# Turning derived token quarters on TensorE instead of by DMA in a fused attention and feed-forward kernel

## What is computed

```python
xn = _layernorm(x)
s = _L0_attn_ref(xn, Wq, Wk, Wv, bias_table, gamma, beta)
h = jnp.square(jax.nn.relu(jnp.einsum('bsd,fd->bsf', xn, W_fc)))
y = jnp.einsum('bsf,df->bsd', h, W_proj)
g = _silu(spikes_counted_over_5_steps(y) / 5)
out = x + s * g
```

## Time and profile before

| | us |
|---|---|
| median of 3 runs | 3989.05 |
| the profiled execution | 3991.72 |
| its span, first to last instruction | 3989.8 |
| TensorE busy (matmul) | 3409.3 (85%) |
| VectorE busy | 2798.7 (70%) |
| ScalarE busy | 2721.0 (68%) |
| GpSimd busy | 1867.6 (47%) |

### The profile page before, as it was taken

How to read it: one execution, slowest core, us unless ns; L and a number is a source line. 1 busy time by engine, 2 the same in 40 slices (tenths; PEclk the granted TensorE clock), 3 DMA queues, 4 the chain that set the end, 5 groups by cost and what they waited for, 6 DMA issues and landing times.

```text
span 3989.8 us, 62988 instructions
## 1 busy us (share of the span) xinstructions
PE 3409.3 (85%) x22284; PEld 1680.2 (42%) x22284; DVE 2798.7 (70%) x4812; ACT 2721.0 (68%) x4411; POOL 1867.6 (47%) x1094
## 2 busy tenths in 40 slices
PE   7566788666667787689999999999999999999996
PEld 4344455444444554445343434343434343434331
DVE  8445666554555665556778788878787888787877
ACT  6233333322223333236999999999999999999997
POOL 4021222121212221115997767576767676767672
PEclk9788898888888888889999999999999999999999
DMA  5544354444443444443132323232323222323232
GB/s 202 152 134 129 108 171 144 138 139 134 141 127 111 145 151 135 140 140 122 38 96 96 112 70 91 91 91 70 112 70 112 71 90 91 91 72 110 71 90 75
DMA packets 334024, 446.07 MB, mean 112 GB/s; under 512 B 175472, under 2 KB 211056, under 8 KB 333712
## 3 DMA queue, kind: packets, MB, share of 16 engines
q1 hardware_dynamic: 315280, 324.61, 27.0%
q10 hardware_dynamic: 18432, 117.45, 8.7%
HBM read 284.75 MB, written 83.95 MB: 92 GB/s over the span
## 4 chain that ended last, share of the span: by engine, by line
ACT 30%; PE 10%; issue 9%; DVE 3%; DMA 1%; SPq 0%; ACTq 0%; POOL 0%; DVEq 0%; POOLq 0%
ACT recurrence_or_probs L1865 16%; ACT s_sb L1872 15%; PE misc L1739 3%; PE acc L1814 2%; PE s_ps L1794 2%; PE s_ps L1780 2%; DVE s_sb L1941 2%; DMA xT<-xnT 1%; PE misc L1721 1%; DVE gate_or_tokens L2070 0%; SPq L319 0%; DVE outT L1961 0%; DVE x_or_queries L1978 0%; DVE gate_or_tokens L2073 0%; PE s_ps L1739 0%
## 5 line engine op out<-in xcount | busy, mean ns | idle before, releaser
L1941 DVE TENSOR_SCALAR_CACHE_REDUCE s_sb<-s_ps 128x1024 f32<-128x1024 f32 x998 | 1214.3, 1221 | 354.2 <-PE s_ps L1780 326.9
L2147 POOL TENSOR_TENSOR recurrence_or_probs<-recurrence_or_probs,toep 128x512 f32<-128x512 f32 (+1 forms) x375 | 1288.8, 3457 | 366.1 <-ACT recurrence_or_probs L1865 365.8
L1872 ACT ACTIVATE s_sb<-s_sb,nmax 128x1024 f32<-128x1024 f32 x998 | 1166.1, 1168 | 9.8 <-DVE s_sb L1941 9.4
L1865 ACT ACTIVATE recurrence_or_probs<-s_ps 128x1024 f32<-128x1024 f32 x1024 | 1060.3, 1037 | 6.8 <-PE s_ps L1794 6.4
L950 ACT ACTIVATE snap<-ps_fc 128x256 f32<-128x256 f32 x384 | 147.5, 384 | 1012.3 <-PE ps_fc L715 1011.0
L732 PE MATMUL ps_y<-w_pr,hid_part 128*128 128x512 f16 x3072 | 831.6, 388 | 0.0
L1814 PE MATMUL acc<-recurrence_or_probs,val 128*32 128x512 f32 x4096 | 545.8, 605 | 1.6 <-DVE recurrence_or_probs L2057 1.5
L715 PE MATMUL ps_fc<-recurrence_or_probs,w_fc 128*128 128x256 f16 x1536 | 224.4, 285 | 240.0 <-DMA recurrence_or_probs<-x_or_queries 209.9
L715 PE MATMUL ps_fc<-xnS_part,w_fc 128*128 128x256 f16 x1536 | 222.7, 284 | 221.5 <-DMA xnS_part<-x_or_queries 184.0
L732 PEld LDWEIGHTS ps_y<-w_pr,hid_part 128*128 128x128 f16 x3072 | 306.7, 100 | 184.0 <-issue 11.3
L1191 DVE BATCH_NORM_STATS2 stats<-x_or_queries 128x6 f32<-128x512 f32 x64 | 40.9, 682 | 488.7 <-DMA x_or_queries<-in_x 488.7
(11 more groups left out here) (202 smaller groups left out, 4388.2 us busy)
## 6 DMA issues: line engine op xcount, KB each, us to landing
w_fc<-fc_made ACTq DMA_DIRECT2D x120, 896.0 KB, 5.1
toep<-table_rows SPq DMA_DIRECT2D x32, 2048.0 KB, 8.4
x_or_queries<-x_or_queries SPq DMA_DIRECT2D x384, 64.0 KB, 2.0
x_or_queries<-in_x SPq DMA_DIRECT2D x16, 1024.0 KB, 6.7
xnT<-xnT_part SPq DMA_DIRECT2D x32, 512.0 KB, 11.8
x_or_gate<-in_x SPq DMA_DIRECT2D x16, 1024.0 KB, 6.6
base<-x_or_gate SPq DMA_DIRECT2D x16, 1024.0 KB, 10.7
xT<-xnT SPq DMA_DIRECT2D x32, 512.0 KB, 9.7
```

Source lines behind the costliest of these rows:

```text
L1865: nc.scalar.activation(prob[:, k % PROBS, 2 * second:2 * second + 2, :].rearrange("p j n -> p (j n)"), s_ps[:, item_buffer(pair_item(m)), ...
L1872: nc.scalar.activation(s_sb[:, i % 4, :], s_sb[:, i % 4, :], ACT.Exp, bias=nmax[:, par, j, st:st + 1], scale=-1.0, accum_out=den[:, par, j ...
L1941: nc.vector.tensor_scalar(s_sb[:, i % 4, :], s_ps[:, item_buffer(tile_item(n)), :], -1.0, None, ALU.mult, ALU.min, accum_out=nmax[:, par, ...
L2147: nc.gpsimd.tensor_tensor(tile, tile, toep[:, par, :, at:at + width], ALU.add).then_inc(biased, 1)
```

## The change

The turns of chunks 1 to 15 are no longer split and then turned by 32 transfers, but turned as float32 by TensorE into the two `ps_t` banks, and split as they are read out of PSUM. A quarter (`turn_quarter`) is four transposes into one bank. Steps 4 and 5 of a chunk take two quarters each for the next chunk (steps 6 and 7 in chunk 0): one ahead of product 2, one ahead of product 5. ScalarE's `copy_turned` writes the hi part straight into `xnS`, in `after_second` and `after_fourth`; VectorE's `turned_lo` the lo part, behind `combine(n, 1)` and behind `combine(n, 2)`. `product(n, 2)` of a chunk waits for these. `take_bank` makes TensorE wait until the last reader of a bank is done. The fetch of x for chunks 2 to 15 moves from SyncE's queue to ScalarE's (`fetch_x`, in `after_second` of step 5, ahead of `snapshot(n, 2)`), where it waits until TensorE has read all four quarters of the chunk before. Turning transfers for `xnT` stay. Left out of the diff: names and semaphores that are only removed.

```diff
--- before.py
+++ after.py
...
 WEIGH_LAG = 3
+TURN_AT = {c * 8 + 4 + 2 * (c == 0) + h: (c + 1, 2 * h) for c in range(15) for h in range(2)}
 FIRST_TILES = 2 * (SLOT_STEPS - TILE_LAG)
...
 QKV_LO_AT = {23: 0, 30: 1, 31: 2}
-TURNS_AT = ({4: (0, 1), 5: (2, 3)}, {3: (0, 1), 4: (2, 3)})
-TURNS_LO_AT = ({5: (0, 1), 6: (2, 3)}, {4: (0, 1), 5: (2, 3)})
 GATES_AT = ({4: (0,), 5: (1,), 6: (2,)}, {4: (0,), 6: (1, 2)})
...
         self.turns = shared[:, 0].rearrange("p a n -> p (a n)").rearrange("p (j t n) -> p j t n", j=4, t=2)
-        self.turn_part = half(1).rearrange("p (a j t n) -> p a j t n", a=2, j=4, t=2)
         self.nat = half(0).rearrange("p (w a s) -> p w a s", w=2, a=2)
...
         turns = first.turns
         xnT = sb("xnT_part", [P, 2, 2, EB, 512], F16)
...
         xn_lo = sem("xn_lo")
         xt_turned = sem("xt_turned")
         xt_stored = sem("xt_stored")
...
                     sp.wait_ge(xs_ps, 4)
-                elif c > 1:
-                    sp.wait_ge(turn_hi, (c - 1) * 4)
-                    sp.wait_ge(turn_lo, (c - 1) * 4)
                 sp.dma_start(x_in[:], d["x"].rearrange("(c t p) e -> c p t e", p=P, t=4)[c]).then_inc(x_loaded, 16)
...
                                          transpose=True).then_inc(xt_turned, 16)
-                if c == 1:
-                    sp.wait_ge(fc_lo, 8)
-                for part, done in ((0, turn_hi), (1, turn_lo)):
-                    for j in range(4):
-                        sp.wait_ge(done, (c - 1) * 4 + j + 1)
-                        for t in range(2):
-                            for k in range(2):
-                                sp.dma_start(xnS[par][:, part, j, k, t * P:(t + 1) * P], turn_part[:, part, j, t, k * P:(k + 1) * P],
-                                             transpose=True).then_inc(xs_turned, 16)
...
                     turn(c + 1, 1 - par)
-                if c < NC - 2:
-                    load_x(c + 2)
                 if c == 0:
...
                     sp.wait_ge(xt_turned, (NC - 1) * TURNED)
-                    sp.wait_ge(xs_turned, (NC - 1) * TURNED)
+                    sp.wait_ge(xs_ps, NC * 4)
                     first.stack(sp, first.nat, first.qst, first.kst)
...
         def _(pe):
+            last_read = [None, None]
+            def take_bank(i):
+                if last_read[i]:
+                    pe.wait_ge(*last_read[i])
+            def turn_quarter(c, j):
+                take_bank(j % 2)
+                pe.wait_ge(turns_made, c * 4 + j + 1)
+                for k in range(2):
+                    for t in range(2):
+                        at = k * HALF + t * P
+                        last = nc.tensor.transpose(ps_t[:, j % 2, at:at + P], turns[:, j, t, k * P:(k + 1) * P], ident[:])
+                last.then_inc(xs_ps, 1)
+                last_read[j % 2] = (xs_lo, c * 4 + j + 1)
             def column_sums(n):
...
                     pe.wait_ge(normed[QKV], 1)
+                if n >= 8:
+                    take_bank(bank[n])
+                    last_read[bank[n]] = (normed[QKV], n - 7)
                 for c in range(4):
...
                 elif i == 2:
-                    if n == 0:
-                        pe.wait_ge(xs_hi, 4)
-                        pe.wait_ge(xs_lo, 4)
-                    elif p == 0:
-                        pe.wait_ge(xs_turned, c * TURNED)
+                    if p == 0:
+                        pe.wait_ge(xs_hi, c * 4 + 4)
+                        pe.wait_ge(xs_lo, c * 4 + 4)
                     pe.wait_ge(snapped, n * 4 + 1)
...
                     pe.wait_ge(first_loaded, 64)
-                wait(pe, first.qk_read, q - 1)
+                take_bank(q % 2)
+                last_read[q % 2] = (first.qk_read, q + 1)
                 which, half = w["q" if q < 2 else "k"], q % 2
...
                 first_tile(n, 0)
+                if n in TURN_AT:
+                    turn_quarter(TURN_AT[n][0], TURN_AT[n][1])
                 product(n, 2)
...
                 proj(b, 1)
+                if n in TURN_AT:
+                    turn_quarter(TURN_AT[n][0], TURN_AT[n][1] + 1)
                 product(n, 5)
...
-            def turned_hi(c, j):
+            def copy_turned(c, j):
                 if j == 0:
-                    act.wait_ge(turns_made, c * 4 + 4)
-                    act.wait_ge(xn_lo, c * 4)
-                nc.scalar.activation(turn_part[:, 0, j], turns[:, j], ACT.Copy).then_inc(turn_hi, 1)
+                    wait(act, multiplied, (c - 1) * PAIRS * PRODUCTS)
+                    if c == 1:
+                        act.wait_ge(fc_lo, 8)
+                act.wait_ge(xs_ps, c * 4 + j + 1)
+                nc.scalar.activation(xnS[c % 2][:, 0, j].rearrange("p k s -> p (k s)"), ps_t[:, j % 2, :], ACT.Copy).then_inc(xs_hi, 1)
+            def fetch_x(c):
+                act.wait_ge(xs_ps, c * 4)
+                nc.scalar.dma_start(x_in[:], d["x"].rearrange("(c t p) e -> c p t e", p=P, t=4)[c]).then_inc(x_loaded, 16)
...
                 if q == 0:
-                    act.wait_ge(turn_lo, (NC - 1) * 4)
+                    act.wait_ge(xs_ps, NC * 4)
                 nc.scalar.activation(first.nat[:, which, 0, half * 512:(half + 1) * 512], ps_t[:, q % 2, :], ACT.Copy,
...
                     spiking.sigmoid(c - 1, p - 3, 1)
+                if n in TURN_AT:
+                    copy_turned(TURN_AT[n][0], TURN_AT[n][1])
+                    if TURN_AT[n][1] and TURN_AT[n][0] < NC - 1:
+                        fetch_x(TURN_AT[n][0] + 1)
                 if n in QKV_AT:
...
                     store_quarters(n + 1)
-                if c < NC - 1 and p in TURNS_AT[c > 0]:
-                    for j in TURNS_AT[c > 0][p]:
-                        turned_hi(c + 1, j)
+                if n in TURN_AT:
+                    copy_turned(TURN_AT[n][0], TURN_AT[n][1] + 1)
                 if n in SQUARE_AT:
...
                         dve.wait_ge(turns_made, 4)
-                    wait(dve, xs_turned, (c - 1) * TURNED)
+                    wait(dve, turns_made, c * 4)
                 nc.vector.tensor_scalar(xn[:, t, :], x_in[:, t, :], mv[:, t, 0:1], rs[:, 6, t:t + 1],
...
             def turned_lo(c, j):
-                dve.wait_ge(turn_hi, (c - 1) * 4 + j + 1)
-                nc.vector.tensor_tensor(turn_part[:, 1, j], turns[:, j], turn_part[:, 0, j], ALU.subtract).then_inc(turn_lo, 1)
+                dve.wait_ge(xs_hi, c * 4 + j + 1)
+                nc.vector.tensor_tensor(xnS[c % 2][:, 1, j].rearrange("p k s -> p (k s)"), ps_t[:, j % 2, :],
+                                        xnS[c % 2][:, 0, j].rearrange("p k s -> p (k s)"), ALU.subtract).then_inc(xs_lo, 1)
...
                     part_lo(c + 1, 1)
-                if ahead and p in TURNS_LO_AT[c > 0]:
-                    for j in TURNS_LO_AT[c > 0][p]:
-                        turned_lo(c + 1, j)
+                if n in TURN_AT:
+                    turned_lo(TURN_AT[n][0], TURN_AT[n][1])
                 if n in QKV_LO_AT:
...
                 combine(n, 2)
+                if n in TURN_AT:
+                    turned_lo(TURN_AT[n][0], TURN_AT[n][1] + 1)
                 if n == 0:
```

More of the change, by code:

```diff
@@ L341, in feed_forward @@
         turns = first.turns
-        turn_part = first.turn_part
         xnT = sb("xnT_part", [P, 2, 2, EB, 512], F16)
@@ L406, in feed_forward @@
         xn_lo = sem("xn_lo")
-        turn_hi = sem("turn_hi")
-        turn_lo = sem("turn_lo")
         xt_turned = sem("xt_turned")
-        xs_turned = sem("xs_turned")
         xt_stored = sem("xt_stored")
```

## The result

The kernel after takes 3522.98 us, the median of four runs (3521.45 to 3525.17), against 3988.62 us of the kernel before beside it (3987.89 to 3991.13): a ratio of 0.8832, 95% interval 0.8817 to 0.8847. That is 465.6 us less. The profiled execution's span is 3521.0 us, 468.8 less than before.

What follows compares the result with a forecast made beforehand. TensorE was taken to be held by waits for transfers into `xnS` at chunk starts. A + B + C = 498 us gained, D + E + F + G = 52 added: 446 less than 3989.05, 3543 us; range 3512 to 3600.

Steps and rivals of the forecast that it cites:

- A: At the start of chunks 1 to 15, TensorE's 15 waits for transfers into `xnS` go: 393.9 us less.
- B: At 14 chunk starts, TensorE's wait behind VectorE's stand for x goes, x being fetched earlier: 54.8 us less.
- C: Behind the idle time at 15 chunk edges, slow matmuls at a lowered clock go: 49.5 us less.
- The 12 us of slack: The 32 `xnT` transfers that stay land some 12 us before the next chunk's product 0 reads them.
- Term D: 16 float32 transposes a chunk on TensorE, 15 chunks, all on the path: 26 us added, upper end 65.
- (1): At product 0 the `xnT` transfers become late, 4 us per chunk plus clock loss: 120 us more, 3663 us; chance 0.09.
- (2): In ScalarE's queue the x fetch holds up weights, or a longer hold costs 5 us a chunk: 3613 us; chance 0.05.
- (3): In step 4 TensorE stands 42 us for GpSimd's turns, 14 times: slower than before, 4131 us; chance 0.02.
- (4): The chunk's edge waits for something else as late as `xnS`: about 3989 us; chance 0.02.
- Term E: In step 5 ScalarE's fetch of x holds snapshot 2 and so product 5: 1.2 us, 14 times, 17 us added.
- Term F: In chunk 1, whose x is fetched together with three weight loads, one wait stays: about 4 us (0 to 10).
- Term G: TensorE's 0.71 us wait behind VectorE's step 4 subtractions may vanish (-15 us) or recur in a second step (+18); taken +5.

Runs made afterwards that it cites:

- turning_16_more: The kernel after with 16 more turning transfers a chunk behind the 32 for `xnT`, product 0 waiting for them too: 3640.17 us, ratio 0.9123.
- x_early_alone: The kernel before with only its fetch of x moved to ScalarE's queue, in step 6 (7 in chunk 0): 3913.69 us, ratio 0.9803.
- fetch_sync: The kernel after with the fetch of x back on SyncE's queue, behind the transfers for `xnT`: 3499.61 us, ratio 0.8767.
- quarters_twice: The kernel after with each quarter turned twice on TensorE, 8 transposes instead of 4: 3548.86 us, ratio 0.8889.
- fetch_late: The kernel after with the fetch of x still on ScalarE's queue, but issued behind snapshot 2 of the step: 3510.01 us, ratio 0.8794.
- turning_8_more: The kernel after with 8 more turning transfers a chunk behind the 32 for `xnT`, product 0 waiting for them too: 3522.39 us, ratio 0.8823.
- before_sub_behind: The kernel before with the second of VectorE's two subtractions moved behind combine 2: 3986.46 us in one run, beside 3988.91 of the kernel before.

## Why the prediction was right, and where it was off

The forecast was 3543 us and the time is 3522.98, 20 us less, inside the range.

**Terms A, B and C** (498.2 us) came as reckoned: no wait for `xnS` or `xnT`, no stand of VectorE for x in chunks 2 to 15, a granted clock of 1.00 at the edges. The 12 us of slack given to `xnT` are some 15: the 32 transfers leave by 605.48 and product 0 starts at 622.07, while in `turning_16_more` product 0 starts 1.3 us behind the end of the last transfer's issue. The prediction counted the landing from that end; the 2.9 us of the earlier trace rows count from the start of the issue. Two reasons were incomplete. The prediction put term B down to the fetch two steps ahead on ScalarE's queue. That is enough by itself (`x_early_alone`), but so is removing the 32 transfers (`fetch_sync`), and the change did both. And C was put down to idle time as a whole; `x_early_alone` shows that about a third of it hung on the second stand. The sum is the same, since both waits went.

**Term D** was 26 us and is 26: the quarters are 0.44 us each on the path by `quarters_twice`. The row of transposes in a row was the right one to take, not the duration of one. The page's 275 ns (the Trainium skill, TensorE: Matmul & The Clock Gate, Part 4: PE-mode transpose) agrees with the 272 to 273 ns of each of the 240 here and says nothing of how closely they follow each other.

**The rivals** stayed away: no wait for `xnT` (1), no row for a weight transfer among the waits of TensorE (2), no wait for the turns (3), and the 15 waits did go (4). 1 and 3 were made to happen above, at 7.0 and 7.5 us a chunk.

**Term E** was 17 us and is 16. ScalarE's timeline at the hold:

```profile
598.98 0.40 ACTq L924 DMA_DIRECT2D x_or_queries<-in_x  x1
599.48 0.38 ACT L960 ACTIVATE snap<-ps_fc 128x256 f32<-128x256 f32 x1 [2.93 <-PE ps_t L627]
```

The fetch is issued as quarter 3 ends, the snapshot follows at 599.48, product 5 at 599.92. Without the hold product 5 would start 0.43 us after the quarter does, at 598.77; it starts 1.15 us later, 14 times. `fetch_late` confirms it: without the hold its chunks are 79.87 us long, 1.15 less.

**Term F** was 4 us and is 8.5. Chunk 1, in TensorE's timeline:

```profile
120.38 0.82 PE L713 MATMUL ps_fc<-recurrence_or_probs,w_fc 128*128 128x256 f16 x6
...
127.33 1.46 PE L713 MATMUL ps_fc<-recurrence_or_probs,w_fc 128*128 128x256 f16 x6 [5.49 <-DVE u L1311]
...
133.39 0.82 PE L713 MATMUL ps_fc<-xnT_part,w_fc 128*128 128x256 f16 x6
```

and in VectorE's, where the statistics wait for x:

```profile
126.26 0.69 DVE L1204 BATCH_NORM_STATS2 stats<-x_or_queries 128x6 f32<-128x512 f32 x1 [7.31 <-DMA x_or_queries<-in_x]
```

The wait is 5.49 us, and the products behind it run slow: from product 2 (120.38) to product 5 (133.39) are 13.01 us, where an undisturbed step has 4.55, so 2.97 are slow matmuls. The prediction counted the wait and left out the clock behind it. x is issued among SyncE's weight loads, as foreseen, and takes 12 us to land instead of the 6.7 of the earlier trace rows; in `turning_8_more`, where these loads leave 10 us later, it lands in 5.9; the transfers' engines are busy all the time there (share 1.00 in the first line of the stretches above). ScalarE's queue:

```profile
114.16 0.46 ACTq L924 DMA_DIRECT2D x_or_queries<-in_x  x1
```

**Term G** is the step that was mis-sized. The prediction took +5 us, between "may shrink to nothing (-15)" and "recur in a second step (+18)". It shrank to nothing: the chunk of 81.02 us is eight steps (78.12), four quarters (1.74) and the hold with its tail (1.15), and nothing more. 14 chunks of 1.16 us are -16. The prediction had one of the two causes, the moved subtraction, and left out the other: TensorE's own added work ahead of product 1 gives VectorE 0.87 us to catch up. The first is shown by `before_sub_behind`; the second follows from its numbers and was not tried alone. The high end, a second pause, had no row behind it.

D + E + F + G = 26 + 16 + 8.5 - 16 = 34.5 instead of 52, and 498.2 - 34.5 = 463.7 us, against 465.6 between the medians and 468.8 between the spans. The 2 to 5 us that remain are not placed. So the 20 us between forecast and result are G (21 us too high), against which F (4.5 us too low) happens to work, and this rest.

## What to carry to other kernels

Work added to the engine that sets the time isn't lost in full where that engine pauses for another one: take the pause off before the addition is counted. A transfer that waits for the engine that sets the time doesn't belong into another engine's program ahead of work for which the first one waits in turn: the same fetch behind that work was 13 us cheaper, and from SyncE's queue, with x of chunk 1 in time as well, 23. And when a queue is shortened, look at what stands behind the removed entries: here the x fetch would have come early by itself (`fetch_sync`).

## What the runs showed of the hardware

- Turning transfers of 32 KB follow each other by 1.3 to 1.4 us in one queue, however few there are (16 in 22.77 us, 8 in 10.22, 32 in 42.37); regular ones of 64 KB took 0.67 us each (24 in 16.00).
- Four float32 transposes of 128 x 128 cost 0.43 us among other matmuls, although each lasts 0.27, and the granted clock stayed at 1.00 with 16 of them in a chunk (540 to 625 us).
- In chunk 6 a second stand of 4 us soon behind one of 26.70 us left the granted clock at 0.56 in the 6.7 us behind it; without it the clock was 0.77 in the first 5.8 us behind the long stand and 1.00 in the next 8. Over 14 chunks such second stands cost 15.5 us of slow matmuls beside their own length.
- VectorE's operations on two operands took 1.76 instead of 0.68 us while GpSimd multiplied beside them. The combine at 588.38, one of whose operands is in PSUM, ran beside the third multiplication and kept its 0.41. The Trainium skill (SBUF — State Buffer, Who interferes with whom) has it that a VectorE instruction with two SBUF inputs and a GpSimd instruction that reads SBUF contend, and that the ports they share are an exclusive lock. The rows agree: the three operations end 0.54 to 0.56 us after the multiplication that began before each.
